# Depthwise convolution and GDN on one core: VectorE begins slot 2 ahead of slot 1's third tap, with fetches and end of program rearranged

## The reference

```python
pooled = x.mean(axis=(2, 3))
t = relu(gamma * (pooled @ w1.T - running_mean) * rsqrt(running_var + EPS) + beta)
wt = (t @ w2.T + b2).reshape(b * DIM, 1, 3, 3) * MASK   # MASK keeps the top row and the left tap
y = depthwise_conv(x, wt, padding=1) + bias             # four taps an image and channel
denom = einsum('nchw,ic->nihw', y * y, gamma_eff) + beta_eff
out = y * rsqrt(denom)
```

## Time and profile before

| | us |
|---|---|
| median of 3 runs | 205.26 (204.66 to 205.92) |
| the profiled execution | 204.76 |
| its span, first to last instruction | 202.9 |
| VectorE busy | 187.9 (93%) |
| TensorE busy | 171.5 (85%) |
| ScalarE busy | 154.1 (76%) |
| GpSimd busy | 150.1 (74%) |
| DMA, mean | 286 GB/s |

### The profile page before, as it was taken

How to read it: one execution, slowest core, us unless ns; L and a number is a source line. 1 busy time by engine, 2 the same in 40 slices (tenths; PEclk the granted TensorE clock), 3 DMA queues, 4 the chain that set the end, 5 groups by cost and what they waited for, 6 DMA issues and landing times.

```text
span 202.9 us, 2970 instructions
## 1 busy us (share of the span) xinstructions
PE 171.5 (85%) x1032; PEld 64.2 (32%) x1032; DVE 187.9 (93%) x189; ACT 154.1 (76%) x177; POOL 150.1 (74%) x85
## 2 busy tenths in 40 slices
PE   0016897779999999798999999999999999989960
PEld 0014442233353434232443333334433323223310
DVE  4899699999999999989999999999999999999990
ACT  2435563969996979799869799999596859599960
POOL 4000033319899999998999999999999999988600
PEclk9999999999999999999999999999999999999997
DMA  5999979916999999999999999975555657377495
GB/s 211 418 411 379 413 267 337 278 43 209 313 323 286 381 342 353 300 359 351 362 300 336 356 373 377 339 285 153 238 166 223 193 212 260 127 264 250 142 335 187
DMA packets 17300, 58.09 MB, mean 286 GB/s; under 512 B 2467, under 2 KB 3110, under 8 KB 17286
## 3 DMA queue, kind: packets, MB, share of 16 engines
q1 hardware_dynamic: 14976, 51.92, 71.0%
q10 hardware_dynamic: 2310, 6.00, 10.6%
HBM read 26.45 MB, written 25.17 MB: 254 GB/s over the span
## 4 chain that ended last, share of the span: by engine, by line
DVE 52%; PE 32%; issue 8%; POOL 3%; DMA 2%; ACT 1%; DVEq 0%
DVE psum L691 28%; PE psum L635 14%; DVE y L691 13%; PE psum L618 10%; DVE part L662 3%; DMA par_s<-in_par 2%; POOL work L744 2%; PE psum L616 2%; DVE work L727 2%; PE psum L584 1%; PE psum L522 1%; POOL work L750 1%; DVE work L721 1%; PE psum L558 1%; PE psum L596 1%
## 5 line engine op out<-in xcount | busy, mean ns | idle before, releaser
L750 POOL TENSOR_TENSOR work<-y,work 128x1024 f32<-128x1024 f32 x44 | 103.6, 2380 | 7.7 <-ACT work L506 7.4
L691 DVE SCALAR_TENSOR_TENSOR psum<-ximg,taps,psum 128x1024 f32<-128x1024 f32 x81 | 104.2, 1286 | 2.8 <-ACT psum L476 0.9
L635 PE MATMUL psum<-work,gam_e 96*32 96x512 f32 x540 | 81.7, 595 | 6.1 <-issue 3.4
L636 PE MATMUL psum<-sqd,gam_e 96*32 96x512 f32 x180 | 81.4, 595 | 0.0
L744 POOL TENSOR_TENSOR work<-y 128x1024 f32<-128x1024 f32 x24 | 45.3, 1899 | 31.8 <-DVE y L691 31.8
L691 DVE SCALAR_TENSOR_TENSOR y<-ximg,taps,psum 128x1024 f32<-128x1024 f32 x47 | 60.2, 1281 | 1.7
L506 ACT ACTIVATE work<-psum,beta_e 128x1024 f32<-128x1024 f32 x45 | 49.7, 1104 | 11.8 <-PE psum L636 11.7
L618 PE MATMUL psum<-ximg,diag 128*128 128x512 f32 x120 | 56.5, 592 | 0.0
L635 PEld LDWEIGHTS psum<-work,gam_e 96*32 96x32 f32 x540 | 21.8, 109 | 60.1 <-issue 57.7
L476 ACT ACTIVATE psum<-ximg,par_s,taps 128x1024 f32<-128x1024 f32 x32 | 38.5, 1202 | 1.2 <-ACT work L484 0.6
L401 ACT ACTIVATE pool_out<-ximg 128x2193 bf16<-128x2193 f32 (+2 forms) x16 | 29.8, 1861 | 7.8 <-DMA ximg<-in_x 7.8
(11 more groups left out here) (78 smaller groups left out, 72.6 us busy)
## 6 DMA issues: line engine op xcount, KB each, us to landing
out_y<-work SPq DMA_DIRECT2D x45, 512.0 KB, 4.0
ximg<-in_x SPq DMA_DIRECT2D x33, 516.0 KB, 6.9
ximg<-in_x SPq DMA_DIRECT2D x11, 580.5 KB, 7.5
sqd<-work ACTq DMA_DIRECT2D x45, 128.0 KB, 4.2
ximg<-in_x SPq DMA_DIRECT2D x3, 451.5 KB, 5.2
out_y<-work SPq DMA_DIRECT2D x2, 384.0 KB, 4.9
out_y<-work SPq DMA_DIRECT2D x4, 192.0 KB, 3.6
ximg<-in_x SPq DMA_DIRECT2D x1, 322.5 KB, 12.2
```

The source lines that it names most:

```text
L635: nc.tensor.matmul(den(n)[own, j:j + BANK], gam_e[:, own], held(n)[0:C, j:j + BANK], start=True, stop=True)
L636: ins = nc.tensor.matmul(den(n)[C:P, j:j + BANK], gam_e[:, s * CD:(s + 1) * CD], sqd[:, t % 2, j:j + BANK], start=True, stop=True)
L691: return nc.vector.scalar_tensor_tensor(out=in_rows(dst), in0=tap_in(n, tap), scalar=tap_w(b, s, tap), in1=in_rows(src), op0=ALU.mult, op1 ...
L750: nc.gpsimd.tensor_tensor(held(n), result(n), held(n), ALU.mult).then_inc(scaled, 1)
```

## The change

**VectorE.** `conv` is cut into three: `begin` (the waits for the base and the taps, first tap), `add_middle` (second tap, where there are three) and `end` (last tap, `convolved`). In the units for which `early_base(t)` holds the order is begin, middle of slot 1, begin of slot 2, end of slot 1, end of slot 2; otherwise it is as before. It holds for u = 2 of the first three images and for all of the last: units 2, 6, 10, 12, 13, 14. In unit 15 begin of block 47 stands ahead of the end of block 46, whose end stands ahead of the middle of 47. `tap_added` becomes a semaphore for each slot, so that `end` waits for its own slot's taps.

**Fetches.** FETCHES has three lists for each turn, and SyncE issues one before each of the three stores. A turn's counts are now 4, 3, 4, 1 instead of 3, 3, 4, 2.

**End.** The second half of `fourth` is cut in two quarters of 256 columns; the denominators of the last go to place 0. The squares of `fourth` move from VectorE to GpSimd, after its last multiply. On SyncE, the store of block 42 goes ahead of the move of the first half of block 47, and the store of block 44 ahead of all the last parts.

```diff
-FETCHES = (((0, 0), (0, 1), (0, 2)), ((1, 0), (1, 1), (1, 2)), ((2, 0), (2, 1), (2, 2), (3, 0)), ((3, 1), (3, 2)))
+FETCHES = ((((0, 0),), ((0, 1), (0, 2)), ((1, 0),)), (((1, 1),), ((1, 2),), ((2, 0),)),
+           (((2, 1),), ((2, 2), (3, 0)), ((3, 1),)), (((3, 2),), (), ()))
...
+    SHORT = HALF // 2
+    LAST_PARTS = ((LAST, 0, N), (LAST + 1, 0, N), (LAST + 2, 0, HALF), (LAST + 2, HALF, N), (FOURTH, 0, HALF),
+                  (FOURTH, HALF, N - SHORT), (FOURTH, N - SHORT, N))
...
-        tap_added = sem("tap_added")
+        tap_added = [sem(f"tap_added{s}") for s in range(SLOTS)]
...
+        def early_base(t):
+            return t % UNITS not in ON_PE and t % UNITS != TAPS_UNIT or t // UNITS == B - 1
...
+        def den_last(k):
+            n, lo, hi = LAST_PARTS[k]
+            return (psum[:, 0] if lo == N - SHORT else den(n))[0:C, lo:hi]
...
+            elif lo == N - SHORT:
+                pe.wait_ge(normed, LAST + 1)
...
-        def conv(dve, n):
+        def begin(dve, n):
             b, u, s = place(n)
-            *first, last = dve_taps(n)
...
-            for k, tap in enumerate(first):
-                add_tap(n, tap, sums(n), sums(n)).then_inc(tap_added, 1)
-                dve.wait_ge(tap_added, dve_adds(n) - len(first) + k + 1)
+            add_tap(n, dve_taps(n)[0], sums(n), sums(n)).then_inc(tap_added[s], 1)
+
+        def add_middle(dve, n):
+            taps_n, s = dve_taps(n), n % SLOTS
+            dve.wait_ge(tap_added[s], dve_adds(n) - len(taps_n) + 2)
+            add_tap(n, taps_n[1], sums(n), sums(n)).then_inc(tap_added[s], 1)
+
+        def end(dve, n):
+            b, u, s = place(n)
+            last = dve_taps(n)[-1]
+            dve.wait_ge(tap_added[s], dve_adds(n))
             if n >= YS:
                 dve.wait_ge(scaled, n - YS + 1)
...
-        def square_fourth(dve, k):
...
+        def square_fourth(pool, lo, hi):
+            n = FOURTH
+            pool.wait_ge(fourth_moved[0], 16 * SLOTS)
+            if lo > 0:
+                pool.wait_ge(fourth_moved[1], 16)
+            wait_stored(pool, n)
+            nc.gpsimd.tensor_tensor(held(n)[0:C, lo:hi], fourth[:, lo:hi], fourth[:, lo:hi], ALU.mult).then_inc(squared_fourth, 1)
...
             for t in range(UNITS_ALL - 1):
-                for b, u, s in fetches(t):
-                    load_next(sp, b, u, s)
-                store(sp, at(t - 2, 1))
-                store(sp, at(t - 2, 2))
-                store(sp, at(t - 1, 0))
+                for k in range(SLOTS):
+                    fetch(sp, t, k)
+                    store(sp, at(t - 2, 1) + k)
...
             move_fourth(sp, LAST + 1)
+            store(sp, LAST - 3)
             move_fourth(sp, LAST + 2, 0, HALF)
-            store(sp, LAST - 3)
             move_fourth(sp, LAST + 2, HALF, N)
             store(sp, LAST - 2)
-            store_last(sp, 0)
             store(sp, LAST - 1)
...
-            for n in range(BLOCKS):
-                conv(dve, n)
+            for t in range(UNITS_ALL - 1):
+                begin(dve, at(t, 0))
+                add_middle(dve, at(t, 0))
+                end(dve, at(t, 0))
+                begin(dve, at(t, 1))
+                add_middle(dve, at(t, 1))
+                if early_base(t):
+                    begin(dve, at(t, 2))
+                    end(dve, at(t, 1))
+                else:
+                    end(dve, at(t, 1))
+                    begin(dve, at(t, 2))
+                end(dve, at(t, 2))
+            begin(dve, LAST)
+            add_middle(dve, LAST)
+            end(dve, LAST)
+            begin(dve, LAST + 1)
+            add_middle(dve, LAST + 1)
+            begin(dve, LAST + 2)
+            end(dve, LAST + 1)
+            add_middle(dve, LAST + 2)
+            end(dve, LAST + 2)
             scale_on_dve(dve, ON_DVE)
-            scale_last(dve, 0)
-            square_fourth(dve, 4)
-            scale_last(dve, 1)
-            square_fourth(dve, 5)
-            for k in range(2, len(LAST_PARTS)):
+            for k in range(len(LAST_PARTS)):
                 scale_last(dve, k)
...
             scale(pool, LAST - 2)
+            square_fourth(pool, 0, HALF)
+            square_fourth(pool, HALF, N)
```

More of the change, by code:

```diff
@@ L209, in dve_adds @@
         def dve_adds(n):
-            return sum(len(dve_taps(k)) - 1 for k in range(n + 1))
+            return sum(len(dve_taps(k)) - 1 for k in range(n % SLOTS, n + 1, SLOTS))
         def on_pool(n):
@@ L349, in load_next, with fetch @@
             load_rows(sp, b + 2, s, u * UR, (u + 1) * UR if u < UNITS - 1 else ROWS, x_loaded[i])
-        def fetches(t):
-            b, k = divmod(t - FETCH_FROM, UNITS)
-            return [(b, u, s) for u, s in FETCHES[k]] if 0 <= b < B - 2 else []
+        def fetch(sp, t, k):
+            b, unit = divmod(t - FETCH_FROM, UNITS)
+            if 0 <= b < B - 2:
+                for u, s in FETCHES[unit][k]:
+                    load_next(sp, b, u, s)
         def store(sp, n):
@@ L510, in rsqrt_last @@
             act.wait_ge(summed, LAST + k + 1)
-            nc.scalar.activation(held(n)[0:C, lo:hi], den(n)[0:C, lo:hi], ACT.Abs_reciprocal_sqrt,
+            nc.scalar.activation(held(n)[0:C, lo:hi], den_last(k), ACT.Abs_reciprocal_sqrt,
                                  bias=beta_e[0:C, 0:1]).then_inc(normed, 1)
@@ L647, in denominators_last @@
                 wait_den_place(pe, n)
+            elif lo == N - SHORT:
+                pe.wait_ge(normed, LAST + 1)
             for j in range(lo, hi, BANK):
-                ins = nc.tensor.matmul(den(n)[0:C, j:j + BANK], gam_e[:, :], held(n)[0:C, j:j + BANK], start=True, stop=True)
+                end = min(j + BANK, hi)
+                ins = nc.tensor.matmul(den_last(k)[:, j - lo:end - lo], gam_e[:, :], held(n)[0:C, j:end], start=True, stop=True)
             ins.then_inc(summed, 1)
@@ L772, in _ @@
             move_fourth(sp, LAST + 1)
+            store(sp, LAST - 3)
             move_fourth(sp, LAST + 2, 0, HALF)
-            store(sp, LAST - 3)
             move_fourth(sp, LAST + 2, HALF, N)
             store(sp, LAST - 2)
-            store_last(sp, 0)
             store(sp, LAST - 1)
-            for k in range(1, len(LAST_PARTS)):
+            for k in range(len(LAST_PARTS)):
                 store_last(sp, k)
@@ L932, in _ @@
             first_base(dve)
-            for n in range(BLOCKS):
-                conv(dve, n)
-            scale_on_dve(dve, ON_DVE)
-            scale_last(dve, 0)
-            square_fourth(dve, 4)
-            scale_last(dve, 1)
-            square_fourth(dve, 5)
-            for k in range(2, len(LAST_PARTS)):
+            for t in range(UNITS_ALL - 1):
[20 more added lines that the diff above has]
+            end(dve, LAST + 2)
+            scale_on_dve(dve, ON_DVE)
+            for k in range(len(LAST_PARTS)):
                 scale_last(dve, k)
```

7 lines of the change are left out of this document (removed).

## The result

| | before | changed kernel |
|---|---|---|
| median, us | 205.22 (6 runs) | 211.88 (6 runs) |
| ratio | | 1.033 (95%: 1.029 to 1.038) |
| profiled span, us | 202.9 | 209.7 |
| VectorE's last block, last tap begins | 188.79 | 195.32 |
| VectorE's last multiply ends | 198.10 | 206.13 |

The change makes the kernel 3.3% slower. The forecast had the sign and less than half the size: 208.2, with 209.8 as the upper end of the range.

The account below looks back on a forecast made before the run. It took VectorE, TensorE and GpSimd to run neck and neck. The last multiply +4.4 us (taps' +2.4 included), stores -1.0, gave +3.4 on 204.76: 208.1, 208.6 on the median's scale, stated as 208.2; range 205.2 to 209.8.

Parts of the forecast that it names:

- part 1: VectorE's taps: beginning slot 2 before slot 1's last tap holds up TensorE and ScalarE; VectorE ends the taps 2.4 us later.
- The sum for the last image: Units 12 to 15: the last block's last tap at 189.96 instead of 188.79, +1.17 us, before the delays of units 6 and 10.
- 1.27 us forecast: Middle units: TensorE's second denominators held by the postponed tap, 0.34 us from unit 6 to 7 and 0.93 from 10 to 11.
- The term for unit 2: Units 2 to 3: a delay of about 0.9 us like unit 10's, counted as nothing.
- the hole at 82.27: A 1.21 us gap in TensorE, waiting for transfers of unit 4; better spread fetches could shorten it and swallow unit 2's delay.
- part 2: Fetches, one at a time between stores: 0 net, or +1.0 us if the moves land 1 us later.
- Rival (b): Fetches don't help and the 128 KB moves land 1 us later: 209.1 us; chance 15%.
- The sign that the forecast gave for part 2: TensorE's gap at 82 us shrinks if the forecast is right.
- Part 3: Program's end: root of 43 slips, GpSimd's squares cost VectorE 1.9 us; last multiply ends at 202.5 against 198.1, +4.4 us.

Follow-up runs that it names:

- fetch_alone: Only the changed fetches, with the old tap order and old end, against the kernel before: 206.42 us, ratio 1.007.
- order_alone: Only VectorE's new tap order, with the old fetches and old end, against the kernel before: 209.45 us, 2.2% above it.
- row3_first: The changed kernel with the piece (3, 0) fetched at the head of turns 4 and 8: 208.77 us, ratio to before 1.020.
- fetch_row3_first_alone: Kernel before with the changed fetches, but piece (3, 0) at the head of turns 4 and 8; old order and end: 204.10 us, ratio 0.991.
- middle_units_only: Changed fetches with piece (3, 0) first, old end, new tap order only in units 2, 6 and 10: 206.98 us, ratio to before 1.006.
- end_alone: Only the new end of the program, with order and fetches as before, against the kernel before: 204.71 us, ratio 1.000.

## Why the prediction was wrong, point by point

**The sign and the mechanism of part 1 were right.** The postponed third tap holds TensorE's second denominators, which start 0.14 us after it. Slot 2 waits for its base. The sum for the last image was 1.17 us; measured 42.06 - 40.92 = 1.14. Units 13 and 14 were forecast at 10.65 and are 10.65. Taking ScalarE's root ahead of the square (10.27) shows that the square ahead of the root accounts for the difference from 10.3. VectorE also waits 0.28 us for ScalarE's base ahead of slot 1 in units 13, 14 and 15; the forecast had that for unit 15 alone (0.38).

**The middle units were mis-sized: 1.27 us forecast, 2.3 to 3.4 measured.** Four pairs of kernels differ in the order of these units and have the same fetches: the changed kernel against fetch_alone (2.25), order_alone against before (2.60), row3_first against fetch_row3_first_alone (2.86) and middle_units_only against the same (3.42). One pair could be scatter, but all four lie above 1.27. The term for unit 2 was counted as nothing, since the hole at 82.27 was to swallow it. In all four pairs units 2 and 3 together are longer, by 0.37 to 1.36 us. Units 6 and 7 were forecast at 0.34 and lost 0.40 in middle_units_only. In unit 10 the forecast took 0.93; units 9, 10 and 11 lost 0.28 + 0.44 + 0.67 = 1.39. What was left out is GpSimd. It was busy 41.6 of 42.3 us; in the new order it stands idle for 2 us ahead of the postponed slot's square (its row at 97.41 in the changed kernel has an idle time of 1.99, the one at 93.81 before 0.59) and has hardly any spare time to make that up. Before ScalarE's root of slot 1 stands its move of slot 1's square, which waits for GpSimd, so the next bases of slot 1 come late as well. The rows of unit 5 under "The middle units" show each step of this. No run takes GpSimd's lag away and leaves the new order, so how much of the 1.0 to 2.2 us beyond the forecast it makes up stays open; the 0.3 us each in units 5 and 9 are the part that the traces trace back to it.

**The step that failed outright is part 2.** It counted the fetches at 0, with +1.0 as the upper bound, "because the early fetch goes into a stretch before the saturated one". Measured, they cost 2.2 us in units 2 to 11 with the old order and 1.9 with the new, and 0.7% of the time (1.5 us) by themselves. The forecast looked at one piece that moved a turn earlier (in fact three do: (1, 0), (2, 0) and (3, 1)) and not at those that moved later within their turn. Of the twelve pieces of an image, five went from the head of their turn to behind a store, which waits for GpSimd's multiply. One of them, (3, 0), had a reader that came as soon as it landed. It should have been held against this reader, ScalarE's sum, for which the profile had the time (79.95) and the landing time. The fetches as changed cost 1.3% against (3, 0) first with the new order in place (1.033 and 1.020), and 1.6% without it (1.007 and 0.991): about 3 us. In row3_first the other four are still behind stores, and the waits are gone.

Rival (b), 209.1, was nearer in its number and named the fetches, but with 128 KB moves that land 1 us later. They don't: the median is 3.4 us in the changed kernel and 4.0 in fetch_alone, before 4.2, and the three moves issued between 74 and 78 us took 5.7 to 6.5 us, before 5.7 to 7.2. The sign that the forecast gave for part 2, a smaller gap of TensorE at 82, says nothing either way. It was 0.36 us in the changed kernel and 1.21 before, but 0.84 and 1.86 in two other kernels with the changed fetches, and 0.17 to 1.21 in those with the old ones.

**Part 3 was right in mechanism and nearly in size.** The forecast had a tail of 202.5 - 191.2 = 11.3 us, measured 10.81. GpSimd and VectorE do block each other, in every kernel in which the squares are on GpSimd; on VectorE all its multiplies of the last parts are back at 1.21 and 0.68. VectorE lost 5.24 - 3.5 = 1.7 us in them, of the 1.9 counted; as it was spared 1.2 us of squares, the net price was 0.49. The larger part of the longer tail, 1.13 us, is the late root of block 43 (order_alone). The root of block 43 slipped behind block 46's square as told: it started at 195.08, 0.24 us before the last block's last tap, where it had been 1.56 before it. The end of the span came 3.6 us after the last multiply, and not 4.8; counted was 1.0 less, it was 1.2.

**The sum.** Forecast +3.4 on the profiled execution, measured 209.7 - 202.9 = +6.8. Taps +6.53 instead of +2.4 (of which 0.9 was already there at unit 2, from the start of the program, as it scatters), tail +1.5 instead of +2.0, after the last multiply -1.2 instead of -1.0. The missing 4.1 us in the taps are the fetches (1.9 to 2.2), the middle units beyond the 1.27 (1.0 to 1.3) and the start (0.9), which is chance. The median, held against the median before, moved by 6.7 us where the forecast had 3.0. The range was too narrow above because it gave an unseen effect of the fetches a bound of one term, worked out from the one transfer that I had looked at.

The Trainium skill's rule on the shared port ("SBUF — State Buffer", "Who interferes with whom"), by which the two instructions exclude each other, agrees with these traces. Here is the end in the changed kernel, all engines in order of time:

```profile
196.25 2.35 POOL L769 TENSOR_TENSOR work<-y,work 128x1024 f32<-128x1024 f32 x1 [0.45 <-ACT work L521]
...
197.22 2.48 DVE L748 TENSOR_TENSOR work<-y,work 128x1024 f32<-128x1024 f32 x1 [0.49 <-ACT work L521]
...
199.09 3.48 POOL L777 TENSOR_TENSOR work<-sqd 96x512 f32<-96x512 f32 x2 [0.48 <-DMA sqd<-y]
...
199.61 5.24 DVE L754 TENSOR_TENSOR work<-y,work 96x1024 f32<-96x1024 f32 x4
```

VectorE's multiply at 197.22 took 2.48 us beside GpSimd's (196.25 to 198.60), and would have taken 1.2: it ended 1.1 us after GpSimd's, as if it had run from 198.6 on. The rows count the time an instruction is blocked as its busy time. That is why a mean duration that grows (1.21 to 2.48) is the sign to look for, not an idle time. That only one of the two instructions runs at a time fits the alternating ends in end_alone and the sums (1.7 us lost for 1.9 us of GpSimd's work); the port itself can't be seen in rows.

## What to carry to other kernels

When an instruction is moved behind another, follow every reader of what it produces, and what stands behind each of these readers in its own queue: a gain of 0.24 us a unit for VectorE cost TensorE 0.8 us of idle time, since it was the sums' last reader that freed the place for other results. When a queue of transfers is rearranged, hold each transfer against its first reader, with the landing time of the profile; one of twelve behind a store instead of ahead of it was the difference between 0.9% of gain and 0.7% of loss. And test the parts of a change apart: here two of the three, each with one thing put right, made a kernel 1.4% faster than before, and the three as they were one that is 3.3% slower.

## What the runs showed of the hardware that was not expected

Where the DMA engines are busy 0.99 of the time, the piece (3, 0) of image 2 took 8.1 us to land in the kernel before, as the last of a burst of four fetches, and 9.1 in the changed one, as the second of two; the first 128 KB move after it took 6.2 and 6.5. From 131 us on, with no fetches left, a move in the kernel before took 2.3 us in the median (2.2 to 3.6).

A VectorE multiply with both inputs in SBUF and a GpSimd square or multiply beside it lengthen each other: 96x1024 took 2.05 us instead of 1.21, 128x1024 took 1.91 and 2.48. The profile counts the time in which one is held as its busy time.

VectorE spaces a tap that waits for its own predecessor 1.32 us, and one that doesn't 1.20. That held unchanged in all kernels, with one instruction in between too, so 0.12 us is what such a wait costs for 1024 columns here.
